# Two of five key chunks of the attention probabilities are turned by VectorE and a DRAM buffer instead of by TensorE

## The reference, cut to what matters

```
scores = jnp.einsum('bqhd,bkhd->bhqk', q, k_all) * SCALE
scores = jnp.where(valid[:, None, None, :], scores, -1e+30)
probs = jax.nn.softmax(scores, axis=-1)
o = jnp.einsum('bhqk,bkhd->bqhd', probs, v_all)
o = o.reshape(bsz, seqlen, HQ * D)
return jnp.einsum('bse,de->bsd', o, Wo)
```

## Time and profile before

| | |
|---|---|
| median of three runs | 1352.56 us |
| span of the profiled execution, first to last instruction | 1349.8 us |
| time of the profiled execution around its span | not shown; the median stands 2.8 us above the span |
| attention, from the first transpose of probabilities to the last | 29.6 to 1080 us |
| TensorE busy | 1342.4 us, 99% of the span, granted clock 1.00 throughout |
| VectorE busy | 1040.8 us, 77% |
| ScalarE busy | 843.2 us, 62% |
| GpSimd busy | 713.6 us, 53% |
| DMA | 168.11 MB, mean 125 GB/s |

### The profile page before, as it was taken

How to read it: one execution, slowest core, us unless ns; L and a number is a source line. 1 busy time by engine, 2 the same in 40 slices (tenths; PEclk the granted TensorE clock), 3 DMA queues, 4 the chain that set the end, 5 groups by cost and what they waited for, 6 DMA issues and landing times.

```text
span 1349.8 us, 24930 instructions
## 1 busy us (share of the span) xinstructions
PE 1342.4 (99%) x7812; PEld 1191.3 (88%) x7812; DVE 1040.8 (77%) x2131; ACT 843.2 (62%) x2217; POOL 713.6 (53%) x972
## 2 busy tenths in 40 slices
PE   9999999999999999999999999999999999999999
PEld 8888888888889998889888989888888888888887
DVE  7988777877787778777877787778778887748546
ACT  7676566666566556666666666566665785545444
POOL 7767465646554655565555555555555652305111
PEclk9999999999999999999999999999999999999999
DMA  5566325522552264126413641364222164354532
GB/s 201 172 185 198 87 82 173 145 63 78 187 127 59 78 201 134 38 84 206 130 31 108 203 109 31 113 210 128 79 48 48 63 191 140 125 183 141 187 141 78
DMA packets 170746, 168.11 MB, mean 125 GB/s; under 512 B 129856, under 2 KB 137664, under 8 KB 159936
## 3 DMA queue, kind: packets, MB, share of 16 engines
q1 hardware_dynamic: 164928, 131.21, 33.3%
q0 software_dynamic: 5760, 36.18, 8.1%
HBM read 133.81 MB, written 33.55 MB: 124 GB/s over the span
## 4 chain that ended last, share of the span: by engine, by line
PE 98%; POOL 1%; DVE 1%; ACT 1%; issue 0%; POOLq 0%; DVEq 0%
PE ps L64 27%; PE ps L63 27%; PE ps L65 27%; PE ps L1131 10%; PE ps L1109 2%; PE ps L1153 1%; PE ps L2038 1%; PE ps L1103 1%; PE ps L2071 0%; PE ps L2070 0%; PE ps L2024 0%; PE ps L2023 0%; PE ps L1332 0%; DVE at_scores L897 0%; PE ps L2009 0%; ACT at_mask L601 0%
## 5 line engine op out<-in xcount | busy, mean ns | idle before, releaser
L502 POOL TENSOR_SCALAR at_probs<-at_probs,at_row_inv 128x640 f32<-128x640 f32 x256 | 211.8, 828 | 151.1 <-DVE at_row_inv L903 150.9
L605 ACT ACTIVATE at_pT_hi<-ps 128x512 fp32r<-128x512 f32 x320 | 186.5, 604 | 101.1 <-PE ps L65 50.9
L897 DVE CUSTOM_DVE_ANT_0 at_scores<-ps,at_mask,at_inv_rms 128x640 f32<-128x640 f32 x256 | 220.2, 879 | 31.7 <-PE ps L65 30.8
L653 ACT ACTIVATE at_probs<-at_scores,at_neg_max 128x640 f32<-128x640 f32 x256 | 211.9, 836 | 51.0 <-DVE at_neg_max L897 51.0
L845 DVE TENSOR_TENSOR at_pT_lo<-ps,at_pT_hi 128x512 fp32r<-128x512 f32 x320 | 212.6, 686 | 25.7 <-ACT at_pT_hi L605 20.7
L63 PE MATMUL ps<-ds_hi,x_hi 128*128 128x512 f32 (+1 forms) x564 | 192.7, 342 | 0.0
L65 PE MATMUL ps<-ds_hi,x_lo 128*128 128x512 f32 (+1 forms) x564 | 192.0, 340 | 0.0
L648 ACT ACTIVATE at_square<-ps 128x128 bf16<-128x128 f32 x256 | 67.1, 276 | 166.7 <-DVE a_raw L876 149.9
L1131 PE MATMUL ps<-ident,at_probs 128*128 128x128 f32 x1280 | 160.6, 273 | 0.0
L63 PE MATMUL ps<-at_kT_hi,ds_lo 128*128 128x320 f32 x512 | 158.1, 309 | 1.6 <-DVE at_neg_max L897 1.6
L65 PE MATMUL ps<-at_kT_hi,ds_lo 128*128 128x320 f32 x512 | 158.2, 309 | 0.0
(11 more groups left out here) (215 smaller groups left out, 3379.6 us busy)
## 6 DMA issues: line engine op xcount, KB each, us to landing
kT_pages<-shared SPq DMA_DIRECT2D x16, 1024.0 KB
kv_raw<-kT_pages SPq DMA_DIRECT2D x60, 256.0 KB, 4.0
v_pages<-shared SPq DMA_DIRECT2D x14, 1024.0 KB
kv_raw<-v_pages SPq DMA_DIRECT2D x56, 256.0 KB, 4.1
sw_wgu_raw<-in_sw_gu SPq DMA_DIRECT2D x22, 512.0 KB, 3.3
staging<-in_L_cond_Wo SPq DMA_DIRECT2D x8, 1024.0 KB, 4.8
staging<-in_L_cond_Wq SPq DMA_DIRECT2D x7, 1024.0 KB
sw_b_raw<-in_sw_bgu SPq DMA_DIRECT2D x88, 64.0 KB, 2.8
```

Source lines behind the costliest of these rows:

```text
L502: pool.tensor_scalar(probs[:, h, :], probs[:, h, :], row_inv[:, h:h + 1], 1.0, ALU.mult, ALU.mult).then_inc(probs_done, 1)
L605: act.activation(out, src, ACT.Copy).then_inc(done, 1)
L653: act.activation(probs[:, h, :], scores[h % 2][:], ACT.Exp, bias=neg_max[:, h:h + 1], scale=-1.0, accum_out=row_sum[:, h:h + 1]).then_inc( ...
L897: dve.tensor_tensor_reduce(out=scores[h % 2][:], in0=slot(h), in1=mask[:, b, :], scale=inv_rms[b % 2][:, h:h + 1], scalar=3.0e38, op0=ALU. ...
```

## The change

In all rounds but the first and the last (`by_moves`), TensorE turns only chunks 0 to 2. Chunks 3 and 4 take another way:

- VectorE, after `normalise` of each head, transposes the 32 x 32 squares of that head's last 256 probabilities (`turn_squares`, one instruction of 128 partitions x 256 elements a head, four a round) into `turned`. For the next round, heads 0 and 1 come before `attended`, head 2 after the last reciprocal and head 3 ahead of the residual's addition.
- SyncE stores `turned` (512 KB) to the DRAM tensor `turned_rows` at the head of its round, waits until it has landed, and reads it back in four DMAs (128 KB each, in runs of 1 KB), which put the squares on their partitions, into `pT_raw`.
- ScalarE and VectorE split chunks 3 and 4 out of `pT_raw`. On ScalarE these two splits now stand behind the exponentials of heads 0 and 1, on VectorE behind the first reciprocal and the second, where before they stood ahead of `turn_k` and `turn_q`.
- TensorE does `score` of heads 2 and 3 ahead of `times_v` of chunks 3 and 4.
- GpSimd's `stage_pages` (the gather of cache pages) moves up, ahead of the rotation of the keys. Some semaphores are merged, and the scratch memory of GpSimd's DMAs is set to 8192.

```diff
+            def by_moves(g, b):
+                return not (isinstance(g, int) and (g, b) in ((0, 0), (HK - 1, B - 1)))
+            def moved_chunk(c):
+                return pT_raw[:, :, c - (KC - MOVED)].rearrange("p a h r -> p h a r")
...
+            def move_turned(g, b):
+                wait_apart(sp, turned_done, upto(g, b, G), passed)
+                sp.dma_start(turned_rows, turned[:].rearrange("p k c h r -> p (k c h r)")).then_inc(pT_moved[b % 2], 16)
+                wait_apart(sp, pT_moved[b % 2], moved_count(g, b) - NQ * 16, passed)
+                for k in range(NQ):
+                    sp.dma_start(pT_raw[k * SQ:(k + 1) * SQ].rearrange("i a c h r -> i a (c h r)"),
+                                 turned_rows.rearrange("(a i) (k n) -> k i a n", a=NQ, k=NQ)[k]).then_inc(pT_moved[b % 2], 16)
...
                 for b in range(B):
                     g2, b2 = following(*following(g, b))
+                    if by_moves(g, b):
+                        move_turned(g, b)
...
@@ ScalarE @@
-                    for c in range(3, KC):
-                        probs_T(g, b, c)
+                    if not by_moves(g, b):
+                        for c in range(KC - MOVED, KC):
+                            probs_T(g, b, c)
...
                     if more:
                         exps(g1, b1, 0)
+                    if by_moves(g, b):
+                        probs_T(g, b, 3)
+                    if more:
                         exps(g1, b1, 1)
+                    if by_moves(g, b):
+                        probs_T(g, b, 4)
+                        exps(g1, b1, 2)
...
@@ VectorE @@
+            def turn_squares(g, b, h):
+                wait_apart(dve, probs_done, upto(g, b, G, h + 1), passed)
+                dve.transpose(turned[:, :, :, h, :].rearrange("p k c r -> p c k r"),
+                              probs[:, h, (KC - MOVED) * P:KEYS].rearrange("p (c k i) -> p c k i", c=MOVED, k=NQ)).then_inc(turned_done, 1)
...
@@ TensorE @@
-                    for c in range(2, KC):
+                    for c in range(2, KC - MOVED if by_moves(g, b) else KC):
                         probs_T(g, b, c)
...
                     times_v(g, b, 2)
-                    times_v(g, b, 3)
-                    if more:
+                    if by_moves(g, b):
                         score(g1, b1, 2)
-                    times_v(g, b, 4)
-                    if more:
                         score(g1, b1, 3)
+                        times_v(g, b, 3)
+                        times_v(g, b, 4)
```

## The result

The changed kernel took 1558.85 us, the median of five runs (1548.18 to 1561.37), against 1352.56 us before (1351.68 to 1353.58): 1.152 times as long, 95% interval 1.148 to 1.155. That is 206 us more, where 64 were forecast. The time lies outside the range. Rival 1 is out. Rival 2 came true beside the forecast. The rest is a longer round than laid out, a stall at each turn of the loop with the slow clock behind it, and two late loads in the last head; none of these was in a step or a rival. The profiled execution is the shortest of the five (1548.18 us), so its rounds are read against 196 us more, and not 206.

A forecast was written before the change was run, and what follows sets the result against it. TensorE's queue alone was taken to set the round. Losses less the gain, +0.86 us over 62 rounds, 53.3, with 8.4 + 1 + 1 gave 63.7 us more: 1416 us, range 1370 to 1465.

The forecast's parts named there:

- Rival 1: Gain kept: TensorE waits only for chunk 0, rounds 0.65 us shorter, 1312 us; chance 0.10.
- Rival 2: Chunks land late beside the gather: chunk 3 1.5 us late in 28 rounds, 42 us more, 1458 us; chance 0.18.
- What TensorE gains: Eight transposes fewer a round on TensorE: 0.87 us a round, 54 us over 62 rounds.
- (a): Chunk 0: TensorE's `times_v` waits for VectorE's `pT_lo`, starts at 2.00 us of the round, 0.22 lost.
- (b): VectorE and ScalarE up to chunk 3: `lo` takes 0.68 us, TensorE starts chunk 3 at 10.92, 0.55 lost.
- (c): Chunk 4: VectorE's `lo` runs 11.70 to 12.39, TensorE starts chunk 4 at 12.44, 0.83 us lost.
- (d): Output: TensorE waits for `oT_lo`, starts `output` at 14.69, 0.13 us lost; the round ends at 17.46.
- The first and sixth rounds of a head: VectorE's weight splits there delay chunk 4 by 0.60 us: 7 + 7 rounds, 8.4 us in all.
- VectorE's transposes: VectorE's new transposes of squares take 0.33 us each, fit in waiting time and cost nothing.
- Rival 3: VectorE's transposes take 0.8 us and push `output` by 0.86: 53 us more, 1470 us; chance 0.06.
- The way over DRAM: Store and reads land at 7.5 us, due at 9.53: 2 us of slack, no cost; upper bound 10.2, 0.7 late.
- I charge nothing: The gather's 1 MB (6.0 us) runs beside store and reads in four rounds of eight, priced at no cost.

The follow-up runs named there:

- e5: Changed kernel without store and reads (constant tile), splits, scores and products in the order of before, squares still transposed: 1350.6 us.
- e2: Changed kernel without the store to DRAM and the four reads; chunks 3 and 4 split from a constant tile: 1490.5 us.
- e1: Changed kernel with only GpSimd's gather of cache pages back behind the rotation of the keys: 1512.6 us.
- e10: e2 with VectorE's transposes of squares left out too, 64 instructions fewer in its loop: 1464.1 us.
- e12: e1 with heads 1 to 6 written out instead of a hardware loop: 1480.7 us.
- e4: Changed kernel with idle transposes on TensorE, 8 ahead of chunk 3's product and 4 ahead of chunk 4's: 1535.2 us.
- e3: Changed kernel with VectorE's reciprocal of head 0 behind the split of chunk 3 instead of ahead of it: 1553.3 us.
- e6: Kernel before with 7 semaphore increments more a round, 56 a pass, on VectorE's list alone: 1370.4 us.
- e9: Kernel before with heads 1 to 6 written out instead of a hardware loop, on all engines: 1352.3 us.
- e8: Changed kernel with only chunk 4 moved, the gather at its old place, chunk 4's split ahead of the first reciprocal: 1414.9 us.

## Why the prediction was wrong, by its steps

The 206 us in steps of one change each, by the medians: transposes off TensorE in the old order, -2 (e5); the new order, +140 (e2 - e5); the way over DRAM, +22 (e1 - e2); the gather moved up, +46 (changed - e1). Across these lie the turn of the loop, 26 to 32 us (e10, e12), and the clock behind gaps, between 24 (e4) and 57.

- **What TensorE gains (-54): mis-sized.** Without the chain behind it the round is 0.45 us shorter (16.15 for 16.60, e5), 28 us over all rounds. TensorE's order was right, but eight transposes less don't take their whole 0.87 us out, since `times_v` of chunk 0 then waits for VectorE. The layout had 0.22 of that in step (a), which would leave 0.65. In e5 it waits longer: VectorE has the transpose of head 3 and the residual ahead, and starts the split of chunk 0 at 1.41 into the round instead of 1.27, so `times_v` starts at 2.14 and not at 2.00. The last 0.06 lies in `times_v` and `project_q` behind it, 4.25 us for 4.18.
- **(a) Chunk 0: right** (2.01 for 2.00).
- **(b) Chunk 3: the mechanism right, one duration wrong.** The step was "VectorE's `lo` of it runs 10.18 to 10.86 (0.68)". It took 1.19 beside GpSimd's multiplication: 0.51 of the 0.58 by which `times_v` of chunk 3 is later than laid out. The 0.68 was read from a split out of PSUM, and an SBUF price beside a busy GpSimd stood in the trace of before (the split of the cached values, 0.77 and more). e3 shows the cause, and e3's 0.35 us is what the order of two instructions was worth.
- **(c) and (d) Chunk 4 and output: right** in size, given (b). Chunk 4 came 1.46 after chunk 3 (laid out: 1.52), `output` 2.38 after that (2.25), and lasted 2.90 (2.77): each of the last two 0.13 more, most of it in the first product behind a gap, which takes 0.50 and not 0.39. In all 0.58 - 0.06 + 0.13 + 0.13 = 0.78, a round of 18.24 for 17.46; 62 x 0.78 = 48 us of the miss.
- **The first and sixth rounds of a head: right** where nothing else is in them (18.7 and 18.9 in heads 7 and 1, 18.8 in three sixth rounds, for 18.24 and the 0.60 laid out).
- **VectorE's transposes: right** (0.42 each, two in 0.74, so about 0.33 apart; 0.33 taken) and free in place. Rival 3 is out. What wasn't seen is that they lengthen VectorE's list in a hardware loop (e6, e10).
- **The way over DRAM: the wrong sentence is "I charge nothing".** Alone it lands in time, as said. Beside a gather the reads take 8.1 us from their issue, past the upper bound (1.5 for the issues and 4.1). The gather's former place, behind the rotation of the keys, was what kept the two apart. Rival 2, at 0.18, has the place and the cause right: with the gather moved back the waits are gone (e1). Its size is near (42 us priced, 46 measured), but in part by luck: it priced 28 rounds at 1.5 us late each, ScalarE waited 1.2 on the mean (33.2 us in all), and the clock, which it did not have, made up the rest. It should have been in the sum: both transfers were on the table, and by its own upper bound there was no slack.
- **Missing altogether:** the 3.4 us stall at the turn of the loop, and the half clock behind gaps. I had forecast gaps of 0.55 and 0.83 us in every round on an engine whose clock had been whole throughout, and never asked what a lower clock would do. The last head's weights and mask, 15 us, are loads on SyncE behind `move_turned`; the prediction named only keys and values there.

The direction, the chain (VectorE and ScalarE from 2% to 24%) and the idle time before `times_v` came as written. Added up over the rounds of the profiled execution, which took 196 us more than before: 64 forecast, + 48 for the longer round, + 43 in the rounds with a gather, + 26 at the turns, + 15 in two rounds of the last head comes to 196. The clock loss is inside these terms, not beside them. The median execution is another 11 us longer; which rounds that lies in isn't known, since only the shortest has a trace.

What stays open: why e3's 0.35 us a round is wholly lost when the gather comes early, and why the same two gaps bring the clock down in some rounds and not in others.

## What to carry to other kernels

Work taken off the busiest engine is won only if what its next instruction waits for comes earlier too: lay out the chain through the other engines first, and price every operand that moves from PSUM to SBUF by a row in which GpSimd works beside it. Where instructions are added inside a hardware loop, count them per engine against its list: 56 more, even empty ones, cost 18 us here, as a stall at each turn. A transfer that is "in time by 2 us" isn't so in rounds where another one starts beside it; give each sort of round its own line in the sum. A wait put at the head of an issuing queue delays every load behind it: here it was two loads that have nothing to do with the change, 15 us.

## What the runs showed of the hardware

- A hardware loop turned for nothing with the old lists (e9 against before), and one cost 3.0 to 3.3 us on VectorE at each turn with 56 instructions more (e6). TensorE stalled about 3 us at each turn in e8.
- After a gap of 3.0 us the granted clock was 0.50 for about 3.4 us. After gaps of 0.90 and 1.11 us in one round it was so in three of six cases, and stayed whole in the other three. Gaps of 0.89 and 0.51 us left it at 1.00 in the quiet round shown.
- A subtraction of two SBUF operands over 512 columns takes 0.68 us alone, and 1.19 when it starts 0.15 us behind GpSimd's multiplication. When it starts first it keeps its 0.67, and the multiplication takes 1.06 for 0.80.
- A transpose of 32 x 32 squares over 128 x 256 floats takes 0.42 us on VectorE.
- 512 KB stored to DRAM landed after 2.6 us; four reads of 128 KB in runs of 1 KB landed 8.1 us after the first issue beside an indirect gather, and within 6.9 in a quiet round.
